# Long filters laid out by pairs of channels, read with a step of two words instead of eight

## The chip, the cores and the metric

The kernel runs on one core of a Trainium2 chip. The metric is the device time of one execution in microseconds (us). Engines are TensorE (PE; its weight loads are listed as PEld), VectorE (DVE), ScalarE (ACT), GpSimd (POOL) and SyncE (SP, which issues the DMAs).

## The reference, cut to what matters

The model is one decoder layer: a gated delta-rule attention with FIR branches, a cross-attention by autocorrelation and a feed-forward block, each followed by a residual sum and a layer norm. Batch is 4, 512 tokens, 256 channels, 4 heads of 64, all float32. The change touches two of the FIR branches:

```python
q, k, v = (silu(_dwconv_causal(x @ w.T, conv)) for ...)       # conv: 4 taps per channel
def fir(x, filt):                                             # one causal filter per channel
    return _dwconv_causal(x.reshape(b, Ll, 256), filt.reshape(256, -1))
short, long_, wide = fir(v, fir_s), fir(v, fir_l), fir(v, fir_wd)   # 3, 31 and 64 taps
delta_out = _delta_rule(q, k, v, beta)                        # chunks with a triangular inverse and a running state
...
o = w0 * short + w1 * long_ + w2 * wide + w3 * delta_out + w4 * v   # gates from statistics of these
```

For every channel, `long_` and `wide` are sums over 31 and 64 earlier tokens with that channel's own taps.

## The kernel before, in words

The program has stages, each a block in which every engine has its own list of instructions; the order within an engine is fixed by hand, and semaphores (`pe.wait_ge(...)` and the like) order the engines among each other. Stage 1 (up to about 57 us in the trace) computes v. Stage 2 (57 to 322 us) holds the long filters and the delta rule. Stages 3 to 5 hold gates, cross-attention and feed-forward.

**Long filters.** A filter becomes a product with a Toeplitz-like matrix: for one channel, the window of 128 values of v (32 windows: 4 batches of 8 blocks of 64 tokens) is the stationary operand, and a matrix of 128 x 64 for each of the two filters is the moving one, 128 columns in all. Row p of this matrix is the filter shifted by p, so the host stores each channel's taps once, padded, as a vector of 191 words, and a DMA with a partition step of one entry fetches the 128 shifted rows (`load_toep`, L301). The vectors lie in memory by pieces of 8 channels, with the 8 channels of one tap side by side. So a partition fetches one run of 64 x 8 words for each filter, and in SBUF the 128 columns of one channel are 8 words apart.

A piece is 8 channels: GpSimd copies the windows of v (`copy_piece`, L1558), TensorE does 8 products in four column groups (`filter_piece`, L810), ScalarE copies the result out of PSUM (`filter_out`, L1175), TensorE turns it to tokens (`to_tokens`, L827), ScalarE copies that to `filtered` (`tokens_out`, L1180). The turning of a piece is issued behind the products of the next one. There are 32 pieces and four buffers for the matrices, so the loads of piece n + 4 are issued when the products of piece n are done (`next_toep`, L730). The first 8 pieces (the opening) have two PSUM banks in turn; later ones share bank 3, and each waits until ScalarE has emptied it.

**Where the pieces stand.** The opening is from 60 to 82 us, among the preparation of batch 0. Then each batch has an inverse of five levels (per level: L921 products, L936 transposes, for batches 0 to 2 a projection of the next batch, L947 products, then VectorE's subtraction L1447) and a recurrence over four chunks, in which the state and the next batch's keys are worked out: L1011 (state times keys), L1464 (VectorE), L770 (updates), L1252 (ScalarE), L1033 (next state), L1468 (VectorE). The recurrences of batches 0, 1 and 2 (about 117 to 140 us, and so on at a distance of 59.7 us) hold 6, 6 and 5 pieces. The last inverse holds 4 in place of the projections, and the last recurrence 3. VectorE's reductions for statistics (L1410, L1413, L1417) fill its time in between. L847, L792 and L424 are other products with 32 stationary and 128 moving columns; their moving operands are contiguous. L853 turns the norms of the next batch's queries.

Level k of the inverse reads, as the moving operand of L921, blocks of 2^k words and skips as many: two and two at the first level (k = 1), 32 in a row at the last.

The two names in the diff that it doesn't print: `hankel(name)` on the host pads the taps and returns `z.reshape(-1, NPIECE, PIECE).transpose(1, 0, 2)`, so the array is (number of groups, 191 taps, channels in a group) and follows `PIECE`; and `D` is 256.

Of the kernel before, what the change touches and what calls it, by code (L numbers as in the profile page):

```python
# [24 lines left out]
P = 128  # L25
B, L, D = 4, 512, 256
H, DK = 4, 64
# [3 lines left out]
NJ = L // DK  # L31
# [5 lines left out]
MF = HID // P  # L37
XH, XD = 16, 16
TOPK = 6
PIECE = 8  # L40
NPIECE = D // PIECE
TOEP_BUFS = 4
HALF = L // 2
BIG = 3.0e38
# [124 lines left out]
def layer(nc, dr, out):  # L169
    ctx = ExitStack()  # L170
    with ctx:
# [26 lines left out]
        v_win = sb("v_win", [P, 2, BT, D])  # L198
# [3 lines left out]
        arena = sb("arena", [P, 30624])  # L202
# [30 lines left out]
        def stat_of(b, n, s):  # L233
# [39 lines left out]
        WL = B * NJ * D  # L273
        filtered = arena[:, 0:WL].rearrange("p (f t c) -> p f t c", f=2, c=D)
        SHORT, DELTA, PLAIN, WIDE, LONG = range(NG)
        TOEP = 2 * DK * PIECE
        toep = [arena[:, WL + i * TOEP:WL + (i + 1) * TOEP].rearrange("p (f c) -> p f c", c=PIECE) for i in range(TOEP_BUFS)]
        A2 = carve(arena, {
            "xT": (KT, L), "kq": (2, 4, L), "k_tok": (2, TT, D), "v_sc": (TT, D),
            "above": (TT, 2, KT, DK), "cross": (TT, 2, KT, DK), "atT": (TT, 2, KT, P), "X": (TT, 2, KT, DK),  # L280
            "XT": (TT, 2, P), "Z": (2, 2, 4, DK // 2), "full": (TT, 2, KT, P),
            "S": (2, KT, P), "ss": (32,), "ks": (16,), "C": (16,), "root": (TT, H), "rn": (2, 2 * TT, H), "th": (16,),
            "v_piece": (2, PIECE, B * NJ), "fir_s": (4, DK)},
            at=WL + TOEP_BUFS * TOEP)

        s2 = signals(2, {
# [6 lines left out]
            "v_copied": 1, "fir_mm": 1, "windows_out": 1, "turn_mm": 1, "fir_out": 1}, ())  # L293
        toep_in = [ctx.enter_context(nc.semaphore(f"toep_in{i}")) for i in range(TOEP_BUFS)]

# [5 lines left out]
        def load_toep(sp, piece):  # L301
            i = piece % TOEP_BUFS
            for f in range(2):
                src = dr[("toep_w", "toep_l")[f]][piece]

                src = bass.AP(src.tensor, src.offset, [[PIECE, P], [1, DK * PIECE]])
                sp.dma_start(toep[i][:, f * DK:(f + 1) * DK, :].rearrange("p f c -> p (f c)"), src).then_inc(toep_in[i], 16)

        at1 = WL + TOEP_BUFS * TOEP + KT * L
        A1 = [carve(arena, {"xT": (KT, L), "acc": (KT, L), "sh": (KT, L), "v_sq": (KT, L), "sh_sq": (KT, L), "rows": (P,)},  # L310
# [356 lines left out]
        tok_of = lambda b: A2["k_tok"][:, b % 2, :, :]  # L667
        norms_of = lambda b, a: A2["rn"][:, b % 2, a * TT:(a + 1) * TT, :]
        OPENING = 8
        FIRST_OF, LAST_LEVELS = (8, 14, 20, 29, NPIECE), range(25, 29)  # L670
        pieces_of = lambda b: range(FIRST_OF[b], LAST_LEVELS[0] if b == B - 2 else FIRST_OF[b + 1])
        fir_bank = lambda n: bank[4 + n % 2 if n < OPENING else 3]
        tok_bank = lambda n: bank[2 + n % 2 if n < OPENING else 3]
# [52 lines left out]
        with nc.Block() as block:  # L726
            @block.sync
            def _(sp):

                def next_toep(piece):  # L730

                    if piece + TOEP_BUFS < NPIECE:
                        sp.wait_ge(s2["fir_mm"].sem, piece + 1)
                        load_toep(sp, piece + TOEP_BUFS)

                for n in range(4):
                    next_toep(n)
                sp.wait_ge(s2["beta_mm"].sem, 1)
                load_keys_xT(sp, 1)
                for n in range(4, OPENING):  # L740
                    next_toep(n)
                for b in range(B):
                    if b + 2 < B:
                        sp.wait_ge(s2["beta_mm"].sem, s2["beta_mm"].at(b + 1, 1))
                        load_keys_xT(sp, b + 2)
                    if b == B - 1:
                        sp.wait_ge(s2["proj"].sem, s2["proj"].at(B - 1, 4))
                        sp.dma_start(first_ctx, dr["ctx"][0].rearrange("(t p) d -> p t d", p=P)).then_inc(first_ctx_in.sem, 16)
                        for n in LAST_LEVELS:
                            next_toep(n)  # L750
                    for n in pieces_of(b):
                        next_toep(n)
                sp.wait_ge(s2["fir_mm"].sem, NPIECE - TOEP_BUFS + 1)
                sp.dma_start(g1x_w, dr["g1x_wT"].rearrange("(k p) n -> p k n", p=P)).then_inc(g1x_in.sem, 16)
                sp.wait_ge(s2["fir_mm"].sem, NPIECE - TOEP_BUFS + 2)
                load_turned_rows(sp, 0)
                sp.wait_ge(s2["fir_mm"].sem, NPIECE)
                for n in ("dft", "idft"):
                    sp.dma_start(late[n].rearrange("p k f -> p (k f)"), dr["c_" + n]).then_inc(late_loaded.sem, 16)
                for n in ("xq_w", "xkv_w", "xo_w"):  # L760
                    sp.dma_start(late[n], dr[n + "T"].rearrange("(k p) n -> p k n", p=P)).then_inc(late_loaded.sem, 16)

            @block.tensor
            def _(pe):
# [35 lines left out]
                def filter_piece(n, first=False):  # L800

                    pe.wait_ge(toep_in[n % TOEP_BUFS], 32 * (n // TOEP_BUFS + 1))
                    pe.wait_ge(s2["v_copied"].sem, n + 1)
                    if n >= OPENING:
                        pe.wait_ge(s2["windows_out"].sem, n)
                        pe.wait_ge(s2["fir_out"].sem, n if first else n - 1)
                    elif n >= 2:
                        pe.wait_ge(s2["windows_out"].sem, n - 1)
                    for c in range(PIECE):
                        i = mm(fir_bank(n)[32 * (c % 4):32 * (c % 4) + 32, (c // 4) * P:(c // 4 + 1) * P],  # L810
                               A2["v_piece"][:, n % 2, c, :], toep[n % TOEP_BUFS][:, :, c], start=True, stop=True)
                    i.then_inc(s2["fir_mm"].sem, 1)
                    if not first:
                        to_tokens(n - 1)

                def to_tokens(n):

                    pe.wait_ge(s2["windows_out"].sem, n + 1)
                    if n == 0:
                        pe.wait_ge(s2["beta_th"].sem, 1)  # L820
                    elif 2 <= n < OPENING:
                        pe.wait_ge(s2["fir_out"].sem, n - 1)
                    for c4 in range(PIECE // 4):
                        for f in range(2):
                            for par in range(2):
                                col = D + f * P + c4 * DK
                                i = mm(tok_bank(n)[half(par), col:col + DK], A2["fir_s"][:, 2 * c4 + f, :],  # L827
                                       const["select"][:, half(par)], start=True, stop=True)
                    i.then_inc(s2["turn_mm"].sem, 1)
# [309 lines left out]
            def _(act):  # L1139
                a = nc.scalar.activation  # L1140

                def square(j):

                    n, k = JOBS[j]
                    if n == DELTA:
                        act.wait_ge(s2["o_out"].sem, s2["o_out"].at(k, TT))
                    else:
                        act.wait_ge(s2["fir_out"].sem, (k + 1) * (NPIECE // H))
                    if j == 7:
                        act.wait_ge(s2["o_out"].sem, s2["o_out"].at(B - 2, TT))  # L1150
                    elif j != 6:
                        act.wait_ge(s2["end_mm"].sem, s2["end_mm"].at(min(j // 2, B - 1), 6))
                    if j == 10:
                        act.wait_ge(s2["job_red"].sem, 8 + 1)
                    a(squares_of(j), rows_of_job(j), ACT.Square).then_inc(s2["squared"].sem, 1)
# [21 lines left out]

                def tokens_out(n):
                    act.wait_ge(s2["turn_mm"].sem, n + 1)
                    nc.scalar.copy(filtered[:, :, :, n * PIECE:(n + 1) * PIECE].rearrange("p f t c -> p f c t"),  # L1180
                                   tok_bank(n)[:, D:2 * D].rearrange("p (f c t) -> p f c t", f=2, c=PIECE))\
                        .then_inc(s2["fir_out"].sem, 1)

                def beta_rows_out(b):
# [130 lines left out]
            def _(dve):  # L1315
# [85 lines left out]
                def job_rows(j):  # L1401
                    n, k = JOBS[j]
                    if n == DELTA:
                        dve.wait_ge(s2["o_out"].sem, s2["o_out"].at(k, TT))
                    else:
                        dve.wait_ge(s2["fir_out"].sem, (k + 1) * (NPIECE // H))
                    return rows_of_job(j)

                def job_sum(j):
# [141 lines left out]
            def _(pool):  # L1551
                g = nc.gpsimd
                give_back(s1.values())

                def copy_piece(n):
                    if n >= 2:
                        pool.wait_ge(s2["fir_mm"].sem, n - 1)
                    g.tensor_copy(A2["v_piece"][:, n % 2, :, :].rearrange("p c (t two) -> p t two c", two=2),  # L1558
                                  v_win[:, :, :, n * PIECE:(n + 1) * PIECE].rearrange("p two t c -> p t two c")).then_inc(s2["v_copied"].sem, 1)

                def k_root(b):
                    pool.wait_ge(s2["c_steps"].sem, s2["c_steps"].at(b, 5))
# [40 lines left out]
                for b in range(B):  # L1603
                    piece = pieces_of(b)
# [1190 lines left out]
```

## Time and profile before

| | us |
|---|---|
| median of 3 runs | 603.6 (602.58 to 607.3) |
| the profiled execution | 605.33 |
| its span in the trace | 603.5 |
| TensorE busy | 534.4 (89%) |
| VectorE busy | 448.0 (74%) |
| ScalarE busy | 260.6 (43%) |
| GpSimd busy | 121.7 (20%) |

The span is what the trace covers; 1.8 us of the profiled execution lie around it. Busy time is the time in which an engine has an instruction in flight. In the timeline, a row gives the start in us, the duration in us (of a merged group, from its first start to its last end), the engine, the line, the operation, the tiles and shapes, and how many instructions are merged; `[0.39 <-PE bank L1033]` says that the engine was idle for 0.39 us before it, until L1033 on TensorE was done. "issue" means a wait that the trace shows no source for.

### The profile page before, as it was taken

How to read it: one execution, taken by the hardware profiler on the slowest of the kernel's cores; microseconds unless marked ns; L12 is line 12 of the kernel's file. 1: busy time of each engine (PE TensorE's matmuls, PEld its weight loads, DVE VectorE, ACT ScalarE, POOL GpSimd, SP SyncE). 2: the span in 40 equal slices, each digit the busy share in tenths (PEclk: the TensorE clock that was granted, in tenths of full speed). 3: DMA queues.
4: the chain of work that ended last, by engine and by line, in shares of the span. 5: the costliest groups of instructions: out<-in, count | busy, mean ns of one | idle time of the engine just before them, and what ended most of it. 6: DMA issues, size and time to landing. Idle time of an engine off the chain costs nothing. (4 is left out here: it accounts for less than half of the span.)

```text
span 603.5 us, 16615 instructions
## 1 busy us (share of the span) xinstructions
PE 534.4 (89%) x7294; PEld 406.0 (67%) x7294; DVE 448.0 (74%) x870; ACT 260.6 (43%) x478; POOL 121.7 (20%) x110
## 2 busy tenths in 40 slices
PE   8876889998999899989788988799999799998993
PEld 4554566767676767677664444478878678787883
DVE  3985867876787678777467799984886968758774
ACT  3665554442444244424245456434333244364441
POOL 1001450071006100611202022205570001000000
PEclk9898979999999999999799998989999999999998
DMA  7600630151015100603153201142000000001102
GB/s 204 241 2 1 202 114 4 38 175 40 3 38 176 39 5 2 206 8 109 37 175 113 69 3 35 36 174 61 27 1 1 1 2 0 1 1 36 35 2 70
DMA packets 26807, 37.48 MB, mean 62 GB/s; under 512 B 4657, under 2 KB 13874, under 8 KB 26735
## 3 DMA queue, kind: packets, MB, share of 16 engines
q1 hardware_dynamic: 26463, 36.16, 18.4%
q8 instruction: 58, 0.95, 0.6%
q10 hardware_dynamic: 272, 0.26, 0.1%
q14 instruction: 14, 0.11, 0.1%
HBM read 34.31 MB, written 2.10 MB: 60 GB/s over the span
## 5 line engine op out<-in xcount | busy, mean ns | idle before, releaser
L320 DVE SCALAR_TENSOR_TENSOR arena<-bank,conv_w,arena 128x511 f32<-128x511 f32 (+2 forms) x72 | 53.2, 746 | 13.8 <-ACT arena L488 10.5
L1558 POOL COPY arena<-v_win 128x256 f32<-128x256 f32 x32 | 20.3, 662 | 166.5 <-PE bank L810 166.5
L1225 ACT COPY arena<-bank 128x512 f32<-128x512 f32 x40 | 21.6, 589 | 45.2 <-PE bank L936 45.2
L810 PE MATMUL bank<-arena 128*32 128x128 f32 x512 | 35.7, 409 | 5.0 <-ACT arena L1175 3.2
L1869 PE MATMUL bank<-v_win,arena 128*128 128x256 f32 x160 | 37.7, 382 | 0.6 <-ACT arena L2125 0.6
L2125 ACT COPY arena<-bank 128x512 f32<-128x512 f32 x38 | 21.6, 583 | 38.2 <-PE bank L1869 28.5
L1180 ACT COPY arena<-bank 128x256 f32<-128x256 f32 x32 | 19.4, 606 | 42.1 <-PE bank L827 42.1
L1869 PEld LDWEIGHTS bank<-v_win,arena 128*128 128x128 f32 x160 | 30.0, 190 | 5.3 <-ACT arena L2125 1.0
L723 PE MATMUL bank<-arena 128*128 128x512 f32 x64 | 31.2, 607 | 0.9 <-PEq L726 0.9
L921 PE MATMUL bank<-arena 64*64 64x32 f32 x1280 | 24.4, 224 | 7.5 <-DVE arena L1447 2.7
L921 PEld LDWEIGHTS bank<-arena 64*64 64x64 f32 x1280 | 21.7, 138 | 10.3 <-DVE arena L1447 6.1
L2259 ACT CAST h_hi<-arena 128x512 fp32r<-128x512 f32 x24 | 14.9, 620 | 30.6 <-DVE arena L2570 30.6
L947 PEld LDWEIGHTS bank<-arena 64*64 64x64 f32 x1280 | 20.7, 136 | 10.3 <-issue 9.8
L827 PEld LDWEIGHTS bank<-c_select,arena 128*64 128x64 f32 x512 | 17.6, 137 | 14.1 <-issue 10.3
L1447 DVE TENSOR_TENSOR arena<-arena,bank 128x128 f32<-128x128 f32 x80 | 18.7, 283 | 10.3 <-PE bank L947 10.3
L1988 PE MATMUL bank<-w_down,h_lo 128*128 128x256 f32 x96 | 23.6, 283 | 2.6 <-DVE arena L2583 2.2
L2689 POOL TENSOR_TENSOR arena<-arena,half_exp 128x8 f32<-128x8 f32 x8 | 12.9, 1636 | 63.9 <-DVE arena L2377 63.9
L810 PEld LDWEIGHTS bank<-arena 128*32 128x32 f32 x512 | 15.3, 121 | 13.8 <-issue 8.2
L2576 DVE TENSOR_TENSOR h_lo<-arena,h_hi 128x512 fp32r<-128x512 f32 x24 | 16.6, 690 | 10.7 <-ACT h_hi L2259 10.7
L827 PE MATMUL bank<-c_select,arena 128*64 128x64 f32 x512 | 22.1, 228 | 1.9 <-ACT arena L1175 1.9
L1988 PE MATMUL bank<-w_down,h_hi 128*128 128x256 f32 x96 | 23.2, 279 | 0.0
L947 PE MATMUL bank<-arena 64*64 64x32 f32 x1280 | 22.9, 221 | 0.0
(306 smaller groups left out, 1411.8 us busy)
## 6 DMA issues: line engine op xcount, KB each, us to landing
arena<-in_toep_w SPq DMA_DIRECT2D x32, 256.0 KB, 3.0
arena<-in_toep_l SPq DMA_DIRECT2D x32, 256.0 KB, 3.7
arena<-in_xT SPq DMA_DIRECT2D x12, 512.0 KB, 4.6
arena<-in_x SPq DMA_DIRECT2D x4, 512.0 KB, 4.2
out<-arena SPq DMA_DIRECT2D x4, 512.0 KB, 2.9
arena<-in_ctx SPq DMA_DIRECT2D x3, 512.0 KB, 3.9
v_win<-in_w_gateT SPq DMA_DIRECT2D x1, 768.0 KB, 5.1
v_win<-in_w_upT SPq DMA_DIRECT2D x1, 768.0 KB, 6.6
```

The costliest lines, as they stand in the source:

```text
L320: return nc.vector.scalar_tensor_tensor(out=acc[:, j:L], in0=src[:, 0:L - j], scalar=conv_w[:, m, CONV_K - 1 - j:CONV_K - j], in1=acc[:, j:L],
L723: return nc.tensor.matmul(hid_bank(b, m)[:], g1x_w[:, k, m * P:(m + 1) * P], A3[b % 2]["xT"][:, k, :], start=(k == 0), stop=False)
L810: i = mm(fir_bank(n)[32 * (c % 4):32 * (c % 4) + 32, (c // 4) * P:(c // 4 + 1) * P], A2["v_piece"][:, n % 2, c, :], toep[n % TOEP_BUFS][:, ...
L827: i = mm(tok_bank(n)[half(par), col:col + DK], A2["fir_s"][:, 2 * c4 + f, :], const["select"][:, half(par)], start=True, stop=True)
L921: i = mm(zw_bank(th, a)[half(p), c:c + DK // 2], A2["above"][half(a), t, e, p, :], x, start=True, stop=True)
L947: i = mm(zw_bank(th, p)[half(a), c:c + DK // 2], A2["XT"][half(p), t, e, half(a)], A2["Z"][half(p), th, a, 2 * t2 + e, :], start=True, sto ...
L1180: nc.scalar.copy(filtered[:, :, :, n * PIECE:(n + 1) * PIECE].rearrange("p f t c -> p f c t"), tok_bank(n)[:, D:2 * D].rearrange("p (f c t ...
L1225: nc.scalar.copy(A2["XT"][:, 2 * th:2 * th + 2, :, :], turn_bank(th)[:].rearrange("p (t e c) -> p t e c", t=2, e=2)).then_inc(s2["xt_out"] ...
L1558: g.tensor_copy(A2["v_piece"][:, n % 2, :, :].rearrange("p c (t two) -> p t two c", two=2), v_win[:, :, :, n * PIECE:(n + 1) * PIECE].rear ...
L1869: i = mm(oo, src[:, k, f * P:(f + 1) * P], w[:, k, :], start=(k == 0), stop=(k == KT - 1 and f > 0))
L1988: i = mm(bank[6 + t // 2][:, (t % 2) * D:(t % 2 + 1) * D], part[:, n % SLOTS, t * P:(t + 1) * P], wd[:, m, :], start=(m == 0 and j == 0 an ...
L2125: nc.scalar.copy(dst(i), bank[RING_FIRST + n % RING].rearrange("p (t c) -> p t c", c=dst(i).shape[-1]))\
```

## The change

`PIECE` now is the number of channels that lie side by side in memory, 2 instead of 8; `BATCHED` takes the old meaning, 8 channels handled at a time. The array in memory is (128 pairs, 191 taps, 2 channels). One DMA of a filter fetches four pairs at once: for each partition four runs of 64 x 2 = 128 words, where it was one run of 512 words. In SBUF the matrix is laid out as (4 pairs, 128 columns, 2 channels), so the 128 columns of one channel are 2 words apart. Its size, the number of DMAs, of products and of all other instructions, and their order, stay as they are.

```diff
-PIECE = 8
+PIECE = 2
 NPIECE = D // PIECE
+BATCHED = 8
+N_BATCHED = D // BATCHED
...
-        TOEP = 2 * DK * PIECE
-        toep = [arena[:, WL + i * TOEP:WL + (i + 1) * TOEP].rearrange("p (f c) -> p f c", c=PIECE) for i in range(TOEP_BUFS)]
+        TOEP = 2 * DK * BATCHED
+        toep = [arena[:, WL + i * TOEP:WL + (i + 1) * TOEP].rearrange("p (g f c) -> p g f c", g=BATCHED // PIECE, c=PIECE) for i in range(TOEP_BUFS)]
...
-                src = dr[("toep_w", "toep_l")[f]][piece]
+                src = dr[("toep_w", "toep_l")[f]][piece * BATCHED // PIECE]
-                src = bass.AP(src.tensor, src.offset, [[PIECE, P], [1, DK * PIECE]])
-                sp.dma_start(toep[i][:, f * DK:(f + 1) * DK, :].rearrange("p f c -> p (f c)"), src).then_inc(toep_in[i], 16)
+                src = bass.AP(src.tensor, src.offset, [[PIECE, P], [(P - 1 + DK) * PIECE, BATCHED // PIECE], [1, DK * PIECE]])
+                sp.dma_start(toep[i][:, :, f * DK:(f + 1) * DK, :].rearrange("p g f c -> p g (f c)"), src).then_inc(toep_in[i], 16)
...
-                    for c in range(PIECE):
+                    for c in range(BATCHED):
                         i = mm(fir_bank(n)[32 * (c % 4):32 * (c % 4) + 32, (c // 4) * P:(c // 4 + 1) * P],
-                               A2["v_piece"][:, n % 2, c, :], toep[n % TOEP_BUFS][:, :, c], start=True, stop=True)
+                               A2["v_piece"][:, n % 2, c, :], toep[n % TOEP_BUFS][:, c // PIECE, :, c % PIECE], start=True, stop=True)
```

Everywhere else in the diff `PIECE` and `NPIECE` are replaced by `BATCHED` and `N_BATCHED`, with the same values as before.

## Rows read from the trace of the kernel before

**Rows 1.** The page, part 1: busy time, share of the span and instructions of each engine.
```profile
PE 534.4 (89%) x7294; PEld 406.0 (67%) x7294; DVE 448.0 (74%) x870; ACT 260.6 (43%) x478; POOL 121.7 (20%) x110
```

**Rows 2.** Details of three lines: durations in ns (min/median/max), first and last start.
```profile
L810 PE MATMUL bank<-arena x512: 390/412/423, 60.1 to 308.1; 128*32 128x128 f32 x171
...
L847 PE MATMUL bank<-arena,c_heads x64: 272/273/420, 61.8 to 241.0; 128*32 128x128 f32 x64
...
L921 PE MATMUL bank<-arena x1280: 186/219/311, 83.3 to 285.1; 64*64 64x32 f32 x183
```

**Rows 3.** Timeline: the first pieces of batch 0's recurrence, and two levels of batch 1's inverse.
```profile
119.94 1.11 PE L810 MATMUL bank<-arena 128*32 128x128 f32 x16
121.17 0.64 PE L847 MATMUL bank<-arena,c_heads 128*32 128x128 f32 x16
...
123.72 0.33 PE L853 MATMUL bank<-c_ident,arena 128*128 128x128 f32 x1 [0.23 <-DVE arena L1352]
...
146.02 0.67 PE L921 MATMUL bank<-arena 64*64 64x32 f32 x32 [0.76 <-DVE arena L1378]
...
165.84 1.14 PE L921 MATMUL bank<-arena 64*64 64x32 f32 x64
```

**Rows 4.** Timeline: batch 0's recurrence from its fourth piece on.
```profile
128.25 1.21 DVE L1410 TENSOR_REDUCE stats<-arena 128x16 f32<-128x1024 f32 x1
...
129.85 0.42 DVE L1468 TENSOR_TENSOR arena<-bank,c_blocks 128x256 f32<-128x256 f32 x1 [0.39 <-PE bank L1033]
...
130.81 0.71 PE L1011 MATMUL bank<-arena 128*128 128x128 f32 x4
...
135.15 0.43 DVE L1468 TENSOR_TENSOR arena<-bank,c_blocks 128x256 f32<-128x256 f32 x1 [1.89 <-PE bank L1033]
...
138.52 0.42 DVE L1464 TENSOR_TENSOR arena<-arena,bank 128x256 f32<-128x256 f32 x1 [1.49 <-PE bank L1011]
```

**Rows 5.** Timeline: the opening.
```profile
63.93 2.91 POOL L1563 TENSOR_TENSOR arena<-arena,half_exp 128x16 f32<-128x16 f32 x1 [1.54 <-DVE arena L1348]
...
69.31 0.61 ACT L1180 COPY arena<-bank 128x256 f32<-128x256 f32 x1 [1.40 <-PE bank L827]
...
73.07 0.69 DVE L1373 TENSOR_TENSOR arena<-bank,c_above 128x512 f32<-128x512 f32 x1 [0.97 <-PE bank L881]
...
75.67 0.65 ACT L1180 COPY arena<-bank 128x256 f32<-128x256 f32 x1 [1.91 <-PE bank L827]
...
81.95 1.38 PE L901 MATMUL bank<-arena 64*128 64x128 f32 x16 [0.90 <-ACT arena L1180]
```

**Rows 6.** Timeline: the last inverse, VectorE before the subtractions of levels 2 and 4.
```profile
272.37 0.95 DVE L1447 TENSOR_TENSOR arena<-arena,bank 128x128 f32<-128x128 f32 x4
...
283.62 0.95 DVE L1447 TENSOR_TENSOR arena<-arena,bank 128x128 f32<-128x128 f32 x4 [0.60 <-PE bank L947]
```

**Rows 7.** Timeline: the last recurrence.
```profile
302.67 1.14 PE L810 MATMUL bank<-arena 128*32 128x128 f32 x16
...
311.37 0.42 DVE L1468 TENSOR_TENSOR arena<-bank,c_blocks 128x256 f32<-128x256 f32 x1 [0.64 <-PE bank L1033]
```

**Rows 8.** Loads: landing of L307's DMAs; the load of x; one issue and its piece.
```profile
DMA to landing us min/median/max: 2.6/3.2/7.8
...
arena<-in_x SPq DMA_DIRECT2D x4, 512.0 KB, 4.2
...
69.07 1.11 SPq L307 DMA_DIRECT2D arena<-in_toep_l  x1
...
77.21 1.11 PE L810 MATMUL bank<-arena 128*32 128x128 f32 x16
```

**Rows 9.** Windows: stretch, its length, busy time of each engine, granted clock, DMA share, GB/s.
```profile
60.00:82.00 22.00, 17.74 (x381) 11.75 (x379) 17.15 (x23) 13.36 (x28) 13.52 (x9) 0.95 0.68 214
82.80:89.60 6.80, 6.80 (x118) 5.96 (x115) 3.34 (x6) 2.52 (x5) 1.29 (x3) 0.50 0.01 2
117.50:139.60 22.10, 20.00 (x346) 14.53 (x345) 16.82 (x28) 10.73 (x23) 11.15 (x7) 1.00 0.51 162
```

More of the change, by code:

```diff
@@ L282, in layer @@
             "S": (2, KT, P), "ss": (32,), "ks": (16,), "C": (16,), "root": (TT, H), "rn": (2, 2 * TT, H), "th": (16,),
[L283 removed]
+            "v_piece": (2, BATCHED, B * NJ), "fir_s": (4, DK)},
             at=WL + TOEP_BUFS * TOEP)
@@ L669, in layer @@
         OPENING = 8
-        FIRST_OF, LAST_LEVELS = (8, 14, 20, 29, NPIECE), range(25, 29)
+        FIRST_OF, LAST_LEVELS = (8, 14, 20, 29, N_BATCHED), range(25, 29)
         pieces_of = lambda b: range(FIRST_OF[b], LAST_LEVELS[0] if b == B - 2 else FIRST_OF[b + 1])
@@ L730, in next_toep @@
                 def next_toep(piece):
-                    if piece + TOEP_BUFS < NPIECE:
+                    if piece + TOEP_BUFS < N_BATCHED:
                         sp.wait_ge(s2["fir_mm"].sem, piece + 1)
@@ L752, in _ @@
                         next_toep(n)
-                sp.wait_ge(s2["fir_mm"].sem, NPIECE - TOEP_BUFS + 1)
+                sp.wait_ge(s2["fir_mm"].sem, N_BATCHED - TOEP_BUFS + 1)
                 sp.dma_start(g1x_w, dr["g1x_wT"].rearrange("(k p) n -> p k n", p=P)).then_inc(g1x_in.sem, 16)
-                sp.wait_ge(s2["fir_mm"].sem, NPIECE - TOEP_BUFS + 2)
+                sp.wait_ge(s2["fir_mm"].sem, N_BATCHED - TOEP_BUFS + 2)
                 load_turned_rows(sp, 0)
-                sp.wait_ge(s2["fir_mm"].sem, NPIECE)
+                sp.wait_ge(s2["fir_mm"].sem, N_BATCHED)
                 for n in ("dft", "idft"):
@@ L822, in to_tokens @@
                         pe.wait_ge(s2["fir_out"].sem, n - 1)
-                    for c4 in range(PIECE // 4):
+                    for c4 in range(BATCHED // 4):
                         for f in range(2):
@@ L1147, in square @@
                     else:
-                        act.wait_ge(s2["fir_out"].sem, (k + 1) * (NPIECE // H))
+                        act.wait_ge(s2["fir_out"].sem, (k + 1) * (N_BATCHED // H))
                     if j == 7:
@@ L1179, in tokens_out @@
                     act.wait_ge(s2["turn_mm"].sem, n + 1)
-                    nc.scalar.copy(filtered[:, :, :, n * PIECE:(n + 1) * PIECE].rearrange("p f t c -> p f c t"),
-                                   tok_bank(n)[:, D:2 * D].rearrange("p (f c t) -> p f c t", f=2, c=PIECE))\
+                    nc.scalar.copy(filtered[:, :, :, n * BATCHED:(n + 1) * BATCHED].rearrange("p f t c -> p f c t"),
+                                   tok_bank(n)[:, D:2 * D].rearrange("p (f c t) -> p f c t", f=2, c=BATCHED))\
                         .then_inc(s2["fir_out"].sem, 1)
@@ L1405, in job_rows @@
                     else:
-                        dve.wait_ge(s2["fir_out"].sem, (k + 1) * (NPIECE // H))
+                        dve.wait_ge(s2["fir_out"].sem, (k + 1) * (N_BATCHED // H))
                     return rows_of_job(j)
@@ L1558, in copy_piece @@
                     g.tensor_copy(A2["v_piece"][:, n % 2, :, :].rearrange("p c (t two) -> p t two c", two=2),
-                                  v_win[:, :, :, n * PIECE:(n + 1) * PIECE].rearrange("p two t c -> p t two c")).then_inc(s2["v_copied"].sem, 1)
+                                  v_win[:, :, :, n * BATCHED:(n + 1) * BATCHED].rearrange("p two t c -> p t two c")).then_inc(s2["v_copied"].sem, 1)
                 def k_root(b):
```

## The prediction, made before the changed kernel was run

> **What bounds the kernel now.** I began with the page: TensorE has work in flight for 89% of the span, more than any other engine [rows 1]. That alone says little, so I went through its groups of products by form and looked up single ones. The products with the long filters (L810: 128 rows, 32 stationary and 128 moving columns) take 412 ns in the median and never under 390. L847, of the same shape and type, takes 273 ns [rows 2]. What differs in the code is the step of the moving operand: 8 words in L810 (`toep[...][:, :, c]`), 1 word in L847.
>
> The timeline gives what one piece costs. A piece is 8 products, recorded as 16 matmuls; from first start to last end it takes 1.11 us, and the 16 matmuls of L847 just behind it take 0.64 us [rows 3]. So reading with a step of 8 words costs 0.47 us a piece, and 32 pieces hold at most 32 x 0.47 = 15.0 us. How much of that is on the path must be read at each place where a piece stands, since every engine has one fixed order with waits between them. The idle times named in the timeline tell it.
>
> **The change, part by part.** The number of products, of DMAs, their bytes and the order of every engine stay. Two things change.
>
> (a) The moving operand steps 2 words instead of 8. No row reads with a step of 2. The upper bound for a piece is today's 1.11 us, the lower 0.64 us; I see no reason for less, nor for more than today. The nearest row is the first level of L921, whose moving operand takes two adjacent words and skips two, so it uses as many of each four words as the new layout: 32 of them take 0.67 us. At the last level, where 32 words in a row are read, 64 take 1.14 us [rows 3]. Less the 0.22 us that one of them lasts [rows 2] both are 14.5 ns each, so half-used memory costs nothing visible there (its weight loads could hide some). By the row at 8 words: a piece is four rounds of four products, so three distances and one duration, (1.11 - 0.41) / 3 = 0.23 us a round, 1.8 ns a column. If that is the price of one fetch, and one fetch now brings two useful words, a column is 0.9 ns, a round 0.12 us and a piece at most 3 x 0.12 + 0.29 = 0.65 us. I take 0.64, a saving of 0.47.
> The Trainium skill, "SBUF — State Buffer", section "SBUF: two separate sides", says that SBUF has lines of 16 bytes and wants at least two hits on each; steps of 32 bytes give one, steps of 8 bytes two. By that rule the step of 2 runs at full rate. The 412 against 273 ns of [rows 2] agree with its first half; no row here tests the second.
>
> What the 0.47 is worth, by place:
> - First two pieces of a recurrence (batches 0 to 2): nothing. The first ends before ScalarE's squares, for which L847 waits; behind the second, L853 starts only when VectorE's copy has ended (0.23 idle) [rows 3].
> - Third and fourth: they stand in a chain through the single PSUM bank (piece, L827, ScalarE's two copies, next piece) to L1033, for which L1468 on VectorE waits 0.39 us [rows 4]. 0.94 is offered. VectorE is busy with its reduction until 129.46, so the state is out at 129.46 + 0.42 = 129.88 instead of 130.27. The next L1011 came at 130.81 in TensorE's own order [rows 4]; now it starts when the state is there, about 129.93: 0.88 of the 0.94 arrives.
> - Fifth and sixth: TensorE runs through, and VectorE waits 1.89 us for L1033 and 1.49 us for L1011 [rows 4]. Late next would be the scaled keys (VectorE's L1362) and ScalarE's copies, both ready in time by my count, with 0.1 us to spare. 0.47 each.
> So 0.88 + 0.94 = 1.82 us in batches 0 and 1 (six pieces), 0.88 + 0.47 = 1.35 in batch 2 (five): 4.99.
> - Opening (eight pieces): the fourth waits for a copy that GpSimd can only make after its power of 2.91 us [rows 5], which swallows what the first three offer. The fourth to sixth are in a chain: ScalarE waits 1.40 us for L827, then VectorE 0.97 for the Gram matrices, then ScalarE 1.91 [rows 5]. 3 x 0.47 = 1.41; the 0.97 covers the 0.94 offered by then. From there to L901, which waits for ScalarE [rows 5], ScalarE is the chain, and the last two pieces give nothing.
> - Last inverse (four pieces): one is hidden, VectorE has no idle time before its L1447 at 272.37. At the other three it waits 0.60 us or more, above 0.47 [rows 6]: 1.41.
> - Last recurrence (three pieces): the first is at the 1.2 GHz level, where the slowest of L847 and of L810 take 420 and 423 ns [rows 2]: 0.05. The other two give 0.47 each; VectorE waits 0.64 at 311.37 [rows 7], so all of it is passed on. After that VectorE is the bound but moves as a whole. 0.99.
> Sum: 4.99 + 1.41 + 1.41 + 0.99 = 8.8 us. What follows stage 2 moves along.
>
> (b) The loads: 512 runs of 512 bytes a DMA instead of 128 of 2 KB. Today they land 3.2 us after issue in the median, 7.8 at most. The nearest row is the load of x, also 512 runs, of 1 KB: 4.2 us [rows 8]. I take 4.2; 3.2 is the lower end, 7.8 the upper. Each load is asked for when the piece four before its own is through: at 69.07 for the piece at 77.21 [rows 8], 8.1 us, some 7 after the change. So I cost it at nothing; without that cover each late piece costs what it is late. On SP's queue the loads of x for later batches stand behind, read 20 us after their issue: covered too. The DMA engines are 68% busy in the opening [rows 9].
> The Trainium skill, "DMA: Bandwidth & Descriptors", section "How a descriptor splits into AXI transactions", speaks against the change: a run that doesn't start on 256 bytes fetches from the boundary below, and here partitions lie 8 bytes apart. By it 2 KB are up to 72 beats and four runs of 512 bytes up to 96; an estimate from that page is a third more transfer time, which the same cover hides.
>
> (c) The clock. TensorE has less in flight: 20.0 of 22.1 us in the first recurrence [rows 9] become some 17.2 of 20.3; 17.7 of 22 in the opening become about 15 of 20.6, and there the clock could fall where it doesn't now. At half the rate each us costs at most 0.5, if TensorE alone is the path; it is so in about half of it, so 0.25. A stretch as long as 82.8 to 89.6, at 0.50 [rows 9], then costs 1.7. I cost it at 0 and keep 2 us each way for the range.
>
> **The rivals.**
> 1. The step of 2 isn't at full rate, or the gain is swallowed between engines. For: no row has that step, and I followed each chain only to its next waits. Against: L921's first level [rows 3] and the idle times of [rows 4 to 7]. Nothing gained gives 603.6; half of 8.8 gives 599.2.
> 2. The loads become late (the slower side). At 68% the engines moved 214 GB/s [rows 9], so 315 when busy, and a pair of 0.52 MB takes 1.7 us. If small, unevenly placed runs take three times that, 5 us, the four pairs asked for from 61.4 on are in at 61.4 + 20 + 3 = 84, where 76 is wanted: 8 us late. The three recurrences and the last inverse would lose 1 or 2 each, some 5 more: 8 + 5 - 8.8 = +4, 608. Waits begin at a landing of 7 us, and the change is slower than before from three times today's cost on. Against: 4.2 us in the nearest row.
> 3. The clock falls in the thinner recurrences. Three times 15 us at 0.25 are 11 us, less 8.8: 606. Against: it is full at 90% in flight [rows 9], and 85% is close to that.
>
> **How the numbers follow.** The profiled execution took 605.33 us, its span 603.5 and 1.8 around it; the sum gives 605.3 - 8.8 = 596.5. It is 1.7 above the median of 603.6, so the median goes to 594.8. Chances: forecast 0.72, rival 1 0.17, rival 2 0.06, rival 3 0.05. The forecast's own range is 592 to 598 (the clock 2 us each way, a few tenths in each chain). To hold 8 in 10 I reach into rival 1: 591.5 to 601. The line of 1% (6 us, about what a measurement of this kernel can tell from no change) lies at 597.6: of the forecast 0.66 is below it. Of rivals 2 and 3 some 0.06 is slower by more than 1% (above 609.6, or near it with a fallen clock). The rest, 0.28, is within.
>
> **What would show it.** L810 near 273 ns in the median and a piece near 0.64 us (rival 1: above 300 ns). The first pieces of batches 0 and 1 start 59.7 us apart now, then 57.9. L901 of the first inverse near 80.5 instead of 81.95; L723, the start of stage 3, near 313.7 instead of 322.48. Both loads land in under 5 us and L810 never waits for a DMA (rival 2: it does, first in the opening). Granted clock 1.00 in the three recurrences (rival 3: 0.50 in part). If L810 is quick and the distance stays 59.7, the path doesn't go through the pieces and my chains are wrong.

## The result, and the profile after

The changed kernel took 596.8 us in the median of 4 runs (595.98 to 598.32), the kernel before 604.0 us beside it (602.58 to 607.3): a ratio of 0.988, interval 0.986 to 0.991, so 1.2% or some 7 us faster. Two later comparisons of the same two kernels (below) gave 0.989 and 0.990. The profiled execution took 596.93 us, its span is 595.1 (605.33 and 603.5 before).

The page and the details of the product's line come first: min/median/max of a matmul's duration in ns, first and last start, and the landing time of the filters' DMAs. Lines of the changed kernel are 2 higher.

```profile
PE 522.4 (88%) x7294; PEld 404.6 (68%) x7294; DVE 447.8 (75%) x870; ACT 260.9 (44%) x478; POOL 123.0 (21%) x110
...
q1 hardware_dynamic: 51039, 36.16, 20.6%
...
L812 PE MATMUL bank<-arena x512: 273/277/423, 58.5 to 299.8; 128*32 128x128 f32 x171
...
DMA to landing us min/median/max: 2.9/3.5/8.1
```

The same instructions as before ([rows 1, 2, 8] answer to them). TensorE's busy time fell by 12.0 us, nearly all of it on this one line: its median went from 412 to 277 ns. But the span fell by 8.4, not 12: some of the shorter products lay beside other work.

The timeline of batch 0's recurrence, against [rows 3] and [rows 4]:

```profile
117.64 0.66 PE L812 MATMUL bank<-arena 128*32 128x128 f32 x16
118.87 0.64 PE L849 MATMUL bank<-arena,c_heads 128*32 128x128 f32 x16 [0.57 <-ACT arena L1208]
120.17 0.63 POOL L1560 COPY arena<-v_win 128x256 f32<-128x256 f32 x1 [0.98 <-PE bank L812]
120.19 0.64 DVE L1345 TENSOR_SCALAR arena<-arena 128x16 f32<-128x16 f32 x1
121.58 0.33 PE L855 MATMUL bank<-c_ident,arena 128*128 128x128 f32 x1 [0.88 <-DVE arena L1354]
124.67 0.66 PE L812 MATMUL bank<-arena 128*32 128x128 f32 x16 [0.64 <-ACT arena L1177]
127.24 0.41 DVE L1470 TENSOR_TENSOR arena<-bank,c_blocks 128x256 f32<-128x256 f32 x1
127.71 0.71 PE L1013 MATMUL bank<-arena 128*128 128x128 f32 x4
129.36 1.29 DVE L1364 TENSOR_TENSOR arena<-arena 128x512 f32<-128x512 f32 x2
130.11 1.25 PE L863 MATMUL bank<-c_ident,arena 128*128 128x128 f32 x8
131.84 0.42 DVE L1470 TENSOR_TENSOR arena<-bank,c_blocks 128x256 f32<-128x256 f32 x1 [1.20 <-PE bank L1035]
134.75 0.42 DVE L1466 TENSOR_TENSOR arena<-arena,bank 128x256 f32<-128x256 f32 x1 [1.03 <-PE bank L1013]
```

A piece takes 0.66 us (1.11 before). The first piece gains the path nothing: TensorE waits for ScalarE before L849, 0.57 us now. Read each event as its time since the first piece. L855 stood at 3.78 and stands at 3.94: 0.16 lost. L1013 stood at 10.87 and stands at 10.07: 0.80 gained, so 0.96 from the third and fourth pieces (0.80, and the 0.16 made good). VectorE then waits for TensorE 1.20 us at the fifth and 1.03 us at the sixth, where it was 1.89 and 1.49; the sixth adds 0.46, the fifth only 0.21. The first pieces of batches 0 and 1 are 58.23 us apart (59.70 before), those of batches 1 and 2 58.35 (59.80).

The end of the opening and three windows (busy time of each engine, then TensorE's granted clock, DMA share, GB/s), against [rows 5] and [rows 9]:

```profile
78.87 2.08 PE L903 MATMUL bank<-arena 64*128 64x128 f32 x16 [0.89 <-ACT arena L1182]
...
60.00:80.50 20.50, 16.55 (x376) 13.33 (x377) 17.06 (x24) 13.28 (x26) 14.99 (x10) 0.83 0.84 233
78.00:84.80 6.80, 5.93 (x90) 5.34 (x92) 3.26 (x5) 3.67 (x7) 3.31 (x4) 0.50 0.25 67
116.00:136.50 20.50, 17.45 (x365) 14.24 (x367) 16.13 (x27) 10.31 (x22) 12.05 (x7) 1.00 0.61 176
```

L903 starts at 78.87 instead of 81.95. Of these 3.08 us, 1.65 were there before the first piece: it starts at 58.50 instead of 60.15. They arise between 24 and 30 us: TensorE's clock was at half in the trace before from 24.7 to 28.1 and wasn't in this one. No product with the filters stands there. The opening itself, first piece to L903, went from 21.80 to 20.37 us: 1.43. The clock is at 1.00 through the recurrence, and stage 3 begins (L725) at 314.05 instead of 322.48.

That the two traces differ by 8.4 us, close to the forecast's 8.8, is in part luck. From stretch to stretch the difference is 1.65 (stage 1), 1.43 (opening), -0.78 (from L903 to the first recurrence), 1.47 + 1.45 + 1.11 (from there to the last inverse), 2.25 (last inverse) and -0.15 (last recurrence). Most of the 2.25 is not the pieces' either: behind the fourth piece of the last inverse the clock was at half for some 8 us in the trace before and for some 1 us in this one.

### The profile page after: what moved, and what is told of

Same layout as the page of the kernel before. It is cut to its first block and busy times, and to the rows that moved or that the text cites. A ratio compares the mean times of both kernels' runs of the same rounds, so it can differ in the third digit from the quotient of the medians.

```text
span 595.1 us, 16615 instructions
## 1 busy us (share of the span) xinstructions
PE 522.4 (88%) x7294; PEld 404.6 (68%) x7294; DVE 447.8 (75%) x870; ACT 260.9 (44%) x478; POOL 123.0 (21%) x110
## 3 DMA queue, kind: packets, MB, share of 16 engines
q1 hardware_dynamic: 51039, 36.16, 20.6%
## 5 line engine op out<-in xcount | busy, mean ns | idle before, releaser
L1560 POOL COPY arena<-v_win 128x256 f32<-128x256 f32 x32 | 21.4, 698 | 158.8 <-PE bank L812 158.7
L923 PE MATMUL bank<-arena 64*64 64x32 f32 x1280 | 24.7, 224 | 8.5 <-DVE arena L1449 3.4
L725 PE MATMUL bank<-arena 128*128 128x512 f32 x64 | 31.2, 609 | 0.9 <-PEq L728 0.9
L949 PEld LDWEIGHTS bank<-arena 64*64 64x64 f32 x1280 | 20.5, 134 | 10.0 <-issue 9.3
L812 PE MATMUL bank<-arena 128*32 128x128 f32 x512 | 23.9, 309 | 3.4 <-ACT arena L1177 2.6
L829 PE MATMUL bank<-c_select,arena 128*64 128x64 f32 x512 | 23.4, 237 | 3.0 <-ACT arena L1177 2.6
L829 PEld LDWEIGHTS bank<-c_select,arena 128*64 128x64 f32 x512 | 18.8, 145 | 9.8 <-issue 6.1
L938 PE MATMUL bank<-c_ident,arena 128*128 128x128 f32 x160 | 23.4, 293 | 0.0
L1427 DVE TENSOR_TENSOR arena<-bank,c_levels 128x256 f32<-128x256 f32 x40 | 16.7, 423 | 8.3 <-PE bank L923 7.6
```

The lines of the kernel that those rows point to most:

```text
L725: return nc.tensor.matmul(hid_bank(b, m)[:], g1x_w[:, k, m * P:(m + 1) * P], A3[b % 2]["xT"][:, k, :], start=(k == 0), stop=False)
L923: i = mm(zw_bank(th, a)[half(p), c:c + DK // 2], A2["above"][half(a), t, e, p, :], x, start=True, stop=True)
L938: i = nc.tensor.transpose(turn_bank(th)[:, c:c + P], A2["X"][:, 2 * th + t2, e, :, :].rearrange("p k c -> p (k c)"), ident[:])
```

## The experiments

**Read alone, loads alone.** The buffer seen as one row of 1024 words, the change is split in two. Read alone keeps the kernel before with its loads, loads alone the changed one with its loads; only the moving operand differs:

```diff
 # read alone, on the kernel before
-   toep[n % TOEP_BUFS][:, :, c]
+   flat[n % TOEP_BUFS].rearrange("p (g f c) -> p g f c", g=4, c=2)[:, c // 2, :, c % 2]
 # loads alone, on the changed kernel
-   toep[n % TOEP_BUFS][:, c // PIECE, :, c % PIECE]
+   flat[n % TOEP_BUFS].rearrange("p (f c) -> p f c", c=8)[:, :, c]
```

> The kernel before with its own loads (runs of 2 KB, eight channels side by side), but products that read with a step of 2 words (other columns than the filter's, so the values of the long filters are not the reference's). Theory: the whole gain is the read: as the changed kernel, ratio to the kernel before 0.985 to 0.990, a piece 0.66 us, starts of batches 0 and 1 58.2 us apart. Rival (the smaller runs of the load cost or give something): its time differs from the changed kernel's by more than 2 us, faster if the small runs hurt.

> The changed kernel with its loads in four runs of 512 bytes, but products that read with a step of 8 words as before (other columns than the filter's, so the values of the long filters are not the reference's). Theory: as the kernel before, ratio 0.997 to 1.003, a piece 1.11 us, 59.7 us between batches 0 and 1; landings up by some 0.3 us and covered. Rival (small runs stall the pieces or the code loading in the opening): slower by 1 us or more, with longer idle times before the products in the opening.

Measured: read alone 598.2 us (10 runs), ratio 0.994 (0.991 to 0.997); loads alone 603.4 (10 runs), ratio 1.001 (0.997 to 1.005). The product's line and the loads' landing, read alone first:

```profile
L811 PE MATMUL bank<-arena x512: 273/276/423, 57.9 to 299.1; 128*32 128x128 f32 x171
...
DMA to landing us min/median/max: 2.6/3.4/8.0
```
```profile
L813 PE MATMUL bank<-arena x512: 390/412/423, 60.0 to 305.7; 128*32 128x128 f32 x171
...
DMA to landing us min/median/max: 2.9/3.5/8.1
```

The distances between the first pieces of the batches are 58.12 and 58.14 us with the quick read alone, 59.68 and 60.30 with the new loads alone (59.70 and 59.80 before). The 60.30 isn't a late piece. Nearly all of its excess stands at one place of batch 1's inverse, where TensorE waits for nothing that the trace shows; the loads alone, then the kernel before:

```profile
234.25 0.21 PE L964 MATMUL bank<-c_ident,arena 64*64 64x64 f32 x1 [0.76 <-issue]
...
233.00 0.21 PE L961 MATMUL bank<-c_ident,arena 64*64 64x64 f32 x1 [0.20 <-issue]
```

This idle time took 0.46 and 0.21 us in two traces of the changed kernel and isn't there in the third, so it varies from execution to execution; whether the loads have a part in it is open. So the gain is the read's, and for the loads no cost to the kernel is shown. The expectation for the read alone (0.985 to 0.990) was missed, though: its ratio is about half a per cent above that of the changed kernel. That the small runs give the difference isn't borne out, since alone they gain nothing. The opening of the read alone took 21.90 us, as much as before, although its first pieces are quick. That returns below.

**Which steps are slow.** On the changed kernel, each piece reads its buffer with a step of its own; the loads stay (the list is written shorter than in the kernel):

```diff
+STEPS = [8]*8 + [1, 2, 3, 4, "pairs of 4", "pairs of 8"] + [5, 6, 7, 8, 4, 2] + [1, 3, "pairs of 8", "pairs of 4", 6] + [2]*7
...
+def moving(n, c):
+    x, k = flat[n % TOEP_BUFS], STEPS[n]
+    if k == "pairs of 4": return x[:, 0:256].rearrange("p (n w) -> p n w", w=4)[:, :, 0:2]
+    if k == "pairs of 8": return x[:, 0:512].rearrange("p (n w) -> p n w", w=8)[:, :, 0:2]
+    return x[:, c % 2:c % 2 + (P - 1) * k + 1:k]
```

> The changed kernel, in which each piece reads its moving operand from the same buffer with a step of its own (the columns are then not those of the filter, so the long filters' values are not the reference's). Opening: 8 words, in every piece. Recurrence of batch 0: 1, 2, 3, 4 words, two adjacent of every 4, two adjacent of every 8. Batch 1: 5, 6, 7, 8, 4, 2. Batch 2: 1, 3, two of 8, two of 4, 6. Later: 2. Theory (one fetch per 16 bytes, two useful words are enough): 1, 2 and both kinds of pairs 0.64 to 0.66 us a piece, 3 between 0.66 and 0.9, everything from 4 on 1.11 us with no difference between 4 and 8. Rival A (the price grows with the memory passed over, 1.8 ns for 32 bytes): 4 words 0.66, 5 about 0.75, 6 about 0.87, 7 about 0.99, 8 1.11, pairs of 8 0.66. Rival B (any step beyond 8 bytes is dear, whatever shares a line): 3 and more 1.11, pairs 1.11 as well.

One run, 601.3 us. The pieces in its timeline: steps 1, 2, 3, 4 (batch 0), then 5 (batch 1), then step 3, pairs of 8 and pairs of 4 (batch 2):

```profile
119.38 0.65 PE L823 MATMUL bank<-arena 128*32 128x128 f32 x16
...
121.16 0.66 PE L823 MATMUL bank<-arena 128*32 128x128 f32 x16
...
124.01 0.88 PE L823 MATMUL bank<-arena 128*32 128x128 f32 x16
...
126.62 1.10 PE L823 MATMUL bank<-arena 128*32 128x128 f32 x16 [0.65 <-POOL arena L1571]
...
177.90 1.13 PE L823 MATMUL bank<-arena 128*32 128x128 f32 x16
...
239.15 0.89 PE L823 MATMUL bank<-arena 128*32 128x128 f32 x16
241.76 0.68 PE L823 MATMUL bank<-arena 128*32 128x128 f32 x16
244.17 0.66 PE L823 MATMUL bank<-arena 128*32 128x128 f32 x16 [0.65 <-ACT arena L1188]
```

Steps 5 to 8 take 1.09 to 1.13 us, as step 4 does. Flat from 4 words on, so the price is not that of the memory passed over; 1.10 at 4 words already, so it is not a threshold at 8. Pairs of words 8 apart pass over as much memory as a step of 4 and are quick. What fits all of them is the number of 16-byte lines that the 128 columns touch: 128 lines from step 4 on, 1.10 us; 96 lines at step 3, 0.88; 64 at step 2 and in both kinds of pairs, 0.66 to 0.68; 32 at step 1, 0.65. That is 0.22 us for each 32 lines above 64; below 64 lines nothing more is gained. The Trainium skill, "SBUF — State Buffer", section "SBUF: two separate sides", asks for two hits on each line; these rows agree, and step 2 stands just at the corner.

**On the path or beside it.** The quick read only in the 19 pieces that the prediction had put on the path, or only in the other 13 (again with the list written shorter):

```diff
+ON_PATH = [3, 4, 5] + [10, 11, 12, 13] + [16, 17, 18, 19] + [22, 23, 24] + [26, 27, 28] + [30, 31]
...
-   toep[n % TOEP_BUFS][:, c // PIECE, :, c % PIECE]
+   (toep[n % TOEP_BUFS][:, c // PIECE, :, c % PIECE] if n in ON_PATH      # "not in" for the other 13
+    else flat[n % TOEP_BUFS].rearrange("p (f c) -> p f c", c=8)[:, :, c])
```

> The changed kernel with the quick read (2 words) only in the 19 pieces that the prediction put on the path: 3 to 5, the third and later ones of the recurrences, the last three of the last inverse, the last two of all. The other 13 read with a step of 8 words (other columns than the filter's, so those channels' values are not the reference's). Theory: the path goes through these alone, so the distance from batch 0 to 1 is at most that of the changed kernel, 58.23 us; since the second piece of a recurrence ends at its old time, GpSimd's copy no longer falls on VectorE's key factors, and it should be 58.07. Opening (first piece to L901's counterpart) 20.4 us as in the changed kernel. Rival (the gain is spread over all pieces): 58.8 to 59.0, opening 21.

> The reverse: the quick read only in the 13 pieces that the prediction called hidden, 8 words in the 19 others (other columns than the filter's there, so those values are not the reference's). Theory: nothing gained; batch 0 to 1 59.7 us, or 59.86 if the second piece's earlier end puts GpSimd's copy on VectorE's key factors as in the changed kernel; opening 21.8. Rival: 59.0 or less and an opening of 21.3.

Measured: path only 594.0 us (591.4 to 600.1), ratio 0.987 (0.980 to 0.995); the other 13 only 603.6 us, ratio 1.000 (0.996 to 1.004). The 13 pieces save 13 x 0.45 = 5.9 us of TensorE's time and nothing of the kernel's that shows: the distances are 59.64 and 59.97, the opening 21.70. The 19 give all of it; path only is even slightly quicker between the batches (58.05 and 58.06 us) than the changed kernel (58.14 to 58.35 in three traces). The timeline of "the other 13 only" says why, GpSimd and VectorE in the first recurrence:

```profile
118.64 0.62 POOL L1563 COPY arena<-v_win 128x256 f32<-128x256 f32 x1 [0.93 <-PE bank L814]
118.71 0.59 DVE L1348 TENSOR_SCALAR arena<-arena 128x16 f32<-128x16 f32 x1
```

VectorE's operation on 16 columns lasts until GpSimd's copy ends (119.30 and 119.26). In the changed kernel it is the same: L1345 took 0.64 us beside L1560. The copy is released by the second piece, and a quicker second piece puts it on a short operation of VectorE's chain. Before, it met another one:

```profile
122.96 0.62 POOL L1558 COPY arena<-v_win 128x256 f32<-128x256 f32 x1 [1.17 <-PE bank L810]
122.98 0.48 DVE L1348 TENSOR_TENSOR arena<-arena 128x16 f32<-128x16 f32 x1
```

This cost 0.3 us then and costs 0.47 now: the 0.16 us lost at L855. The Trainium skill, "SBUF — State Buffer", section "Who interferes with whom", describes such a lock between the two engines' shared ports; the two ends that fall together here agree with it.

**The copy later.** GpSimd waits for the end of VectorE's short chain before it copies:

```diff
 if b < B - 1:
+    pool.wait_ge(s2["c_steps"].sem, s2["c_steps"].at(b + 1, 5))
     copy_piece(piece[3])
     k_root(b + 1)
```

> The changed kernel, but GpSimd makes the copy for the fourth piece of a recurrence only when VectorE is through with the next batch's key factors. Theory: in the changed kernel this copy runs beside VectorE's short operation on 16 numbers, which takes 636 ns instead of 175; apart from each other both go quickly, and what stands behind it (key factors, norms, L1013, the reductions) comes 0.46 us earlier: distance 57.8 us, time down by 1.4 us over three batches. Rival (the 636 ns have another reason): the short operation stays at 0.5 us or more, distance 58.2 or more.

Measured: 595.6 us (4 runs), ratio 0.989 (0.983 to 0.994). The distances are 57.76 and 57.75 us, 0.4 to 0.6 less than in the changed kernel, and both short operations are short:

```profile
120.09 0.17 DVE L1345 TENSOR_SCALAR arena<-arena 128x16 f32<-128x16 f32 x1
...
120.59 0.17 DVE L1350 TENSOR_TENSOR arena<-arena 128x16 f32<-128x16 f32 x1
...
120.83 0.66 POOL L1560 COPY arena<-v_win 128x256 f32<-128x256 f32 x1 [1.72 <-DVE arena L1350]
```

Two batches of 0.4 to 0.6 and 0.4 in the third are some 1.3 us; the medians can't tell that from nothing, the distances can.

**The keys first.** The fifth piece passed on 0.21 of 0.45 us. Behind it TensorE turns the scaled keys (L863), and VectorE makes them (L1364) behind a reduction and two other steps. In the first recurrence L1364 starts 11.72 us after the first piece (before, its line 1362, 12.04), and L863 spreads to 1.25 us, where it takes 1.09 elsewhere:

```profile
131.98 1.28 DVE L1362 TENSOR_TENSOR arena<-arena 128x512 f32<-128x512 f32 x2
```

The edit takes one reduction out from in front of the keys:

```diff
 state_out(b, 1)
 if more:
-    job_largest(j + 1)
+    k_scale(b + 1, 0)
+    k_scale(b + 1, 1)
 output_out(b, 1)
 rest(b, 2)
 if more:
-    k_scale(b + 1, 0)
-    k_scale(b + 1, 1)
+    job_largest(j + 1)
```

> The changed kernel with one move on VectorE: in the recurrences of batches 0 to 2 the two scalings of the next batch's keys come before the reduction of a maximum that stood ahead of them, and that reduction comes behind the third chunk's difference. Theory: the fifth piece gave 0.2 us instead of 0.45 because the turning back of the keys waited for these scalings; with them early the distance between batches 0 and 1 falls from 58.2 to about 58.0 us, and the time by 0.5 to 0.8 us against the changed kernel. Rival (the turning waited for something else, or the difference in state now comes late): distance 58.2 or more, no gain.

Measured: 595.7 us (593.7 to 601.6, 9 runs), ratio 0.988 (0.985 to 0.992); distances 58.05 and 58.06, 0.1 to 0.3 less than in the traces of the changed kernel, where the fifth piece lacks 0.24. The direction is as expected. But the keys aren't all that holds back the fifth piece. First the changed kernel, then this run, behind the fifth piece:

```profile
129.03 0.41 DVE L1466 TENSOR_TENSOR arena<-arena,bank 128x256 f32<-128x256 f32 x1
129.49 0.69 PE L772 MATMUL bank<-arena 128*64 128x64 f32 x16
...
131.19 0.61 PE L1035 MATMUL bank<-arena 128*128 128x128 f32 x4
```
```profile
134.24 0.69 PE L772 MATMUL bank<-arena 128*64 128x64 f32 x16
134.85 1.09 PE L863 MATMUL bank<-c_ident,arena 128*128 128x128 f32 x8
135.78 0.61 PE L1035 MATMUL bank<-arena 128*128 128x128 f32 x4
```

From L863's start to L1035's it was 0.93 us in the trace before, is 1.08 in the changed kernel and 0.93 again with the keys first: 0.15 of the 0.24 is the keys. The other 0.09 stands in front of L863: L772 starts 0.05 us after the end of L1466, which VectorE, busy with a reduction and another operation, reaches late. With the keys first this wait grows to 0.16, so only 0.08 of the 0.15 arrives.

**Both moves.** The last two edits together, and the changed kernel once more beside them:

> The changed kernel with both moves, the scalings of the keys early on VectorE and GpSimd's copy behind the key factors. Theory: the two gains stand at different places of the recurrence and add: distance 57.75 less 0.15 to 0.2, so 57.55 to 57.6 us; over three batches 1.8 to 2.0 us below the changed kernel, ratio to it 0.997. Rival (both take away the same wait): 57.75, no more than the late copy alone.

Measured: 594.6 us (591.9 to 597.5, 6 runs), ratio 0.985 (0.981 to 0.989). The distances are 57.67 and 57.70, between the expectation and its rival: with the copy out of the way, the keys first give 0.09 and 0.05 more, about the 0.08 above. This version is quicker than the kernel before; against the changed one the medians of that comparison differ by 3.0 us, of which the distances explain some 1.5, and the intervals of the two ratios overlap.

**The changed kernel, twice more.** No edit; the question was why the quick read alone had an opening of 21.90 us.

> The changed kernel once more, beside the others on the same chip. Theory: distances 58.2 and 58.35 us again, since the gain sits in the order of the pieces; between runs only the stretches at the low clock and stage 1 move, so single times spread over several us. Ratio to the kernel before 0.985 to 0.990. Rival (part of the 8.4 us between the two traces was chance, not the pieces): ratio 0.990 to 0.995 and distances that differ from the first trace's by more than 0.2.

> The changed kernel a third time, beside the two moves and the kernel before on the same chip, for the ratio: theory 0.986 to 0.990 against the kernel before, and a trace whose opening takes 20.4 us at full clock or 21.9 with a stretch at the low clock in it, nothing between; distances 58.15 to 58.35. Rival (the opening's length depends on something else, such as late loads): 21 us or more with the clock full, or an idle time before the products put down to a DMA.

Measured: 596.2 us (592.9 to 597.6), ratio 0.989 (0.982 to 0.996), and 597.6 (592.9 to 599.6), ratio 0.990 (0.986 to 0.994). The first of the two has an opening of 21.90 us. In its timeline the fourth piece is that at 64.94:

```profile
64.20 2.41 POOL L1560 COPY arena<-v_win 128x256 f32<-128x256 f32 x3
...
64.94 0.66 PE L812 MATMUL bank<-arena 128*32 128x128 f32 x16 [1.89 <-issue]
...
66.15 1.94 PE L863 MATMUL bank<-c_ident,arena 128*128 128x128 f32 x8
...
68.02 1.08 PE L812 MATMUL bank<-arena 128*32 128x128 f32 x16
...
69.03 0.94 PE L829 MATMUL bank<-c_select,arena 128*64 128x64 f32 x16
```

The same place in the first trace of the changed kernel:

```profile
65.14 2.43 POOL L1560 COPY arena<-v_win 128x256 f32<-128x256 f32 x3
...
65.87 0.66 PE L812 MATMUL bank<-arena 128*32 128x128 f32 x16 [0.77 <-issue]
...
67.08 1.09 PE L863 MATMUL bank<-c_ident,arena 128*128 128x128 f32 x8
```

and one window of the one and then of the other:

```profile
66.00:69.60 3.60, 3.60 (x42) 2.79 (x40) 3.50 (x4) 2.00 (x4) 1.02 (x2) 0.53 0.64 162
```

```profile
66.00:69.60 3.60, 3.60 (x90) 2.88 (x86) 3.60 (x5) 2.90 (x6) 2.20 (x3) 1.00 0.91 228
```

With quick pieces TensorE reaches the fourth sooner and waits there. The trace names no source for this wait; in the code it is GpSimd's copy, held back by its power, and the piece starts 0.74 and 0.73 us after the copies do. It is 1.89 us of idle time, and 1.2 us after it the clock falls to half (0.53 in the window, the level of 1.2 GHz) on the chain through ScalarE. L863 is 0.85 us longer, the fifth piece 0.42, L829 0.25: 1.52 together, and the opening is 1.53 longer. In the other trace the clock was at half from 54.0 to 64.2 instead; the first pieces took 1.08 us, TensorE came later and idled 0.77, and the clock was full behind it. Of the eight traces with quick path pieces three have this second fall (read alone, changed again, both moves: 21.85 to 21.90 us), all behind an idle time of 1.89; the openings of the other five took 20.37 to 20.69. The idle time alone doesn't do it: the run with the later copy has the same 1.89 us there, at full clock behind it, and took 20.37, and the other 13 only has 1.88 and no fall. What decides is open. In the traces with slow path pieces (before, loads alone, the other 13 only) the fall never came, and they took 21.70 to 21.81. The third trace of the changed kernel gave 20.69, between the only two values that I had expected: its clock fell at 77 us already, under the last turning of the opening (L829, 0.98 instead of 0.69 us).

The changed kernel can have such an opening too, so this doesn't explain why the median of the read alone is higher; that stays open.

The last inverse has a second such place. One window of the first trace of the changed kernel, then of the second:

```profile
268.60:272.20 3.60, 3.60 (x46) 2.80 (x46) 2.68 (x3) 1.17 (x2) 0.43 (x1) 0.56 0.03 8
...
268.60:272.20 3.60, 2.92 (x75) 2.43 (x74) 2.46 (x3) 1.29 (x3) 0.64 (x1) 1.00 0.19 55
```

From the first to the fourth piece of the last inverse it takes 16.31 us in the one and 14.91 in the other. This fall stands in three of the eight traces with quick path pieces (first, third, both moves: 15.69 to 16.31 us) and in none with slow ones (15.38 to 15.65).

## Why the prediction was right

The time was forecast at 594.8 us, the range was 591.5 to 601, and 596.8 was measured. The mechanism was that of the forecast; its sum, 8.8 us, was 1.6 to 3 us above what the medians of three comparisons differ by (5.8 to 7.2). Term by term:

- **The price of a piece.** 0.47 us expected, 0.45 measured: 1.11 to 0.66, just above the 0.65 that I had as the most. Right, and why is shown by the run with one step for each piece. That half-used memory costs nothing, as I had read from L921, is shown by the pairs of words.
- **First two pieces of a recurrence: nothing.** Right in that nothing is gained; the run with the other 13 alone shows it for all hidden pieces. Missed: the second piece releases GpSimd's copy, and 0.16 us is lost where it meets VectorE.
- **Third and fourth: 0.88.** Measured 0.96, with the gate that I had named, VectorE's state before L1013 (L1013 starts 0.06 us after L1470 ends).
- **Fifth and sixth: 0.94.** This is the step that was mis-sized. I took the scaled keys to be "ready in time by my count, with 0.1 us to spare". The sixth gave 0.46, the fifth 0.21: 0.15 went to the keys and 0.09 to L1466 on VectorE, which I hadn't looked at. So a batch gave 1.47 and 1.45 us, not 1.82 (1.51 to 1.66 in the two later traces), and batch 2, up to the first piece of the last inverse, 1.1 and not 1.35: 4.0 to 4.3 in place of 4.99.
- **Opening: 1.41.** Measured 1.43 between the first two traces; 1.0 to 1.4 over the five traces without a second fall. I had said that "there the clock could fall where it doesn't now", priced it at 1.7 and kept it for the range. It falls in three traces of eight and costs 1.5, which is all of the term.
- **Last inverse: 1.41.** From its first to its fourth piece, which holds two of the three path pieces, it took 15.38 to 15.65 us in three traces with slow pieces and 14.64 to 14.91 in four with quick ones, all at full clock there: 0.5 to 1.0, around the middle 0.7 of 0.94. In three others the clock fell there and nothing is gained (15.69 to 16.31), which I hadn't foreseen. The rest, up to the last recurrence, has stretches of half clock in every trace with quick pieces and can't be told apart, so the third path piece isn't shown.
- **Last recurrence: 0.99.** From its first piece to stage 3 it takes 19.7 to 19.8 us before and with the loads alone, 18.8 to 18.9 in the four traces with full clock behind the first piece: 0.9. In the four others the three pieces lie at half clock or nearly so; there it takes 19.8 to 20.5, 19.96 in the first trace of the changed kernel, and nothing is gained.
- **The loads: nothing.** Right. They land after 3.5 us in the median; I had taken 4.2, and the maximum is 8.1, but TensorE never waited for one. They do cost the DMA engines: queue 1 took 18.4% of 603.5 us before and 20.6% of 595.1 now, 111 and 123 us, so 10% more for all its transfers (8% between the read alone and the changed kernel, 19.0% of 595.8 us and the same 123). The filters are 16.8 of the 36.16 MB, so by bytes this would be some 18 to 22% more for them, an estimate. The Trainium skill's count of beats ("DMA: Bandwidth & Descriptors", "How a descriptor splits into AXI transactions"), from which I estimated a third more, points the right way and is the upper side.
- **The median.** The trace before was 1.7 us above its median, which I took off. The terms as measured are 1.0 to 1.4, 4.0 to 4.3 and 0.9, and for the last inverse 0.7, or 1.1 if the third piece gives as much as the two, so 6.6 to 7.7 us where the clock holds. The medians differ by 5.8 to 7.2. I had costed the clock at nothing, and it takes back the opening's term in three traces of eight, the last inverse's in three and the last recurrence's in four. That this is what the medians lack fits, but where the clock falls only a profiled execution shows.

The rivals: that step 2 isn't at full rate is excluded by the 277 ns. Late loads: no wait of the pieces on a DMA shows, and their idle time without a named source didn't grow (9.8 us before, 6.8 in the first trace, 9.9 with the loads alone). The clock in the recurrences of batches 0 to 2: 1.00 in all of them.

## What to carry to other kernels

When an operation gets faster, count it by its place: 19 of 32 equal pieces gave the whole gain here, and the other 13, sped up alone, nothing. Follow what the faster operation releases on the engines off the path as well: here it was GpSimd's copy, and holding it back by one wait gave more between the batches than reordering the path did. A margin of a tenth in a chain of estimated times is no margin; take only part of such a term.

## What the runs showed of the hardware

TensorE's fp32 moving operand is priced by 16-byte lines: 128 columns in 128, 96 and 64 lines take 1.10, 0.88 and 0.66 us a piece, and beyond a step of 4 words nothing more is lost. A copy of 128 x 256 on GpSimd makes a VectorE operation on 16 columns last 0.48 to 0.64 us instead of 0.17. A fall to the level of 1.2 GHz in the opening costs 1.5 us; it stood behind an idle time of 1.89 us three times, and two other times an idle time of 1.88 or 1.89 had none.
